# Q and K of a window-attention kernel as three fp32r products each, with the rounding on GpSimd

## The reference, cut to what matters

```python
x = _L0_conv_ref(x, ...)                     # 1x1, grouped 3x3, 1x1 convolution, residual, relu
y = _ln(x, norm1_w, norm1_b)                 # per position, over 128 channels
win = ...                                    # rolled by 3, cut into windows of 7 x 7 = 49 positions
qkv = (win @ qkv_w.T).reshape(B * nW, N, 3, h, d).transpose(2, 0, 3, 1, 4)    # 8 heads of 16
q, k, v = (qkv[0], qkv[1], qkv[2])
attn = jnp.einsum('bhnd,bhmd->bhnm', q, k) * scale + bias + mask
attn = jax.nn.softmax(attn, axis=-1)
out = jnp.einsum('bhnm,bhmd->bhnd', attn, v) @ proj_w.T + proj_b
x = shortcut + out
z = _ln(x, norm2_w, norm2_b)
return x + jax.nn.gelu(z @ fc1_w.T + fc1_b, approximate=False) @ fc2_w.T + fc2_b
```

## Time and profile before

| | |
|---|---|
| median of three runs | 4525.73 us |
| the profiled execution, its own time | 4518.32 us |
| its span in the profile | 4516.2 us |
| PE busy, share of the span | 98% |
| ACT, DVE, POOL busy | 76%, 70%, 49% |
| granted PE clock, mean | 0.992 |

### The profile page before, as it was taken

How to read it: one execution, slowest core, us unless ns; L and a number is a source line. 1 busy time by engine, 2 the same in 40 slices (tenths; PEclk the granted TensorE clock), 3 DMA queues, 4 the chain that set the end, 5 groups by cost and what they waited for, 6 DMA issues and landing times.

```text
span 4516.2 us, 192181 instructions
## 1 busy us (share of the span) xinstructions
PE 4423.1 (98%) x71190; PEld 3178.5 (70%) x71190; DVE 3178.4 (70%) x7717; ACT 3415.4 (76%) x5644; POOL 2207.9 (49%) x3242
## 2 busy tenths in 40 slices
PE   8999996999999999999999999999999999999998
PEld 5666665677777777777777777777777777777775
DVE  4444444777777777777777777777777777777775
ACT  3444443888888888888888888888888888888886
POOL 4444442455554545455555555455555545455553
PEclk9999998999999999999999999999999999999999
DMA  4545442011111111111111111111111111111110
GB/s 138 153 151 163 151 153 66 25 30 29 29 29 30 30 29 29 29 30 29 29 29 30 30 29 29 29 30 29 29 29 29 29 29 29 30 30 29 29 29 26
DMA packets 298330, 218.64 MB, mean 48 GB/s; under 512 B 43377, under 2 KB 245518, under 8 KB 298190
## 3 DMA queue, kind: packets, MB, share of 16 engines
q1 hardware_dynamic: 294632, 215.41, 16.4%
q10 hardware_dynamic: 3558, 1.07, 0.1%
HBM read 110.73 MB, written 111.94 MB: 49 GB/s over the span
## 4 chain that ended last, share of the span: by engine, by line
PE 97%; DVE 1%; issue 1%; ACT 0%; POOL 0%; DMA 0%; DVEq 0%; POOLq 0%; ACTq 0%
PE bank L666 16%; PE bank L608 10%; PE bank L585 8%; PE bank L509 6%; PE bank L576 6%; PE bank L641 6%; PE bank L657 6%; PE bank L595 6%; PE bank L567 5%; PE bank L620 5%; PE bank L522 5%; PE bank L631 4%; PE bank L659 4%; PE bank L658 4%; PE bank L673 2%; PE bank L487 2%
## 5 line engine op out<-in xcount | busy, mean ns | idle before, releaser
L1234 POOL TENSOR_TENSOR sc<-sc,mx 128x784 f32<-128x784 f32 x512 | 779.2, 1522 | 940.9 <-DVE mx L1068 940.9
L666 PE MATMUL bank<-g,fc_sb 128*128 128x392 f32 x2048 | 785.4, 506 | 0.1
L1221 POOL TENSOR_TENSOR res<-x,projb 98x512 f32<-98x512 f32 x256 | 326.3, 1275 | 804.2 <-DVE x L1104 804.2
L861 ACT ACTIVATE g<-bank,fc1b 128x392 f32<-128x392 f32 x1024 | 560.6, 592 | 172.6 <-PE bank L659 172.6
L1087 DVE SCALAR_TENSOR_TENSOR xn<-x,lnp 98x128 f32<-98x128 f32 x1024 | 292.8, 349 | 491.1 <-POOL lnp L1157 491.1
L608 PEld LDWEIGHTS bank<-ident_sb,sc 128*113 128x113 f32 x4096 | 495.6, 177 | 113.1 <-DVE shared L1038 109.8
L666 PEld LDWEIGHTS bank<-g,fc_sb 128*128 128x128 f32 x2048 | 348.7, 190 | 306.2 <-issue 163.1
L608 PE MATMUL bank<-ident_sb,sc 128*113 128x128 f32 x4096 | 547.8, 277 | 0.1
L1062 DVE TENSOR_TENSOR sc<-bank,shared 128x392 f32<-128x392 f32 x1024 | 528.7, 560 | 2.8 <-PE bank L595 2.8
L1068 DVE TENSOR_REDUCE mx<-sc 128x16 f32<-128x784 f32 x512 | 496.6, 970 | 18.5
L1157 POOL TENSOR_TENSOR lnp<-lnp,half 98x8 f32<-98x8 f32 x518 | 467.7, 924 | 20.3
(11 more groups left out here) (105 smaller groups left out, 8258.3 us busy)
## 6 DMA issues: line engine op xcount, KB each, us to landing
x<-x_scratch SPq DMA_DIRECT2D x768, 49.0 KB
out_x<-y SPq DMA_DIRECT2D x672, 49.0 KB
xc_even<-in_x SPq DMA_DIRECT2D x128, 196.0 KB
shared<-in_x SPq DMA_DIRECT2D x128, 196.0 KB
x_scratch<-xc_even SPq DMA_DIRECT2D x128, 196.0 KB
x_scratch<-shared SPq DMA_DIRECT2D x128, 196.0 KB
x<-x_scratch SPq DMA_DIRECT2D x256, 38.5 KB
out_x<-y SPq DMA_DIRECT2D x224, 38.5 KB
```

Source lines behind the costliest of these rows:

```text
L666: mm = nc.tensor.matmul(RC[:, 0:ST], fc2[:, c, :], g[:, c], start=c == 0, stop=c == HC - 1)
L861: nc.scalar.activation(g[:, j], ring[:, 0:ST], ACT.Gelu, bias=fc1b[:, j:j + 1]).then_inc(out_, 1)
L1234: P.tensor_tensor(out=s_r, in0=s_r, in1=m_r.to_broadcast([128, 2 * HEADS, N]), op=ALU.subtract).then_inc(sub_done, 1)
```

## The change

- The normed input `xt` gets a high part `xt_hi`, rounded to fp32r by POOL (`xt_round`, a multiplication by one), and a low part `xt_lo = xt - xt_hi` by DVE (`xt_rest`). The weights of Q and K get theirs once, in the preparation.
- K and Q are three fp32r products each: high by high, low weight by high, high weight by low.
- V is still one fp32 product from `xt`. On PE it moves ahead of K; K moves behind the transposition of z, and Q follows right behind K, into bank 0 of the scores, which is free then. DVE takes Q out of there.
- On ACT, V goes ahead of `zt_hi`, K behind it, and the first two gelu go ahead of the first two pieces of the probabilities.

```diff
-        A_JOBS = 3
+        A_JOBS = 2
...
             def values(t, j):
 
                 if j == 0:
+                    pe.wait_ge(a_out, A_JOBS * t.n + 1)
                     wait(pe, b_out[0], 5 * t.n - 3)
...
-            def project(t, i):
-
-                part = 1 - i
-                wait(pe, a_out, A_JOBS * t.n + 1 + i)
-                nc.tensor.matmul(RA[:, 0:ST], wqkv[:, C * part:C * part + C], xt[:],
-                                 start=True, stop=True).then_inc(a_full, 1)
+            def split_product(dst, part):
+                cols = slice(C * part, C * part + C)
+                nc.tensor.matmul(dst, wqk_hi[:, cols], xt_hi[:], start=True, stop=False)
+                nc.tensor.matmul(dst, wqk_lo[:, cols], xt_hi[:], start=False, stop=False)
+                return nc.tensor.matmul(dst, wqk_hi[:, cols], xt_lo[:], start=False, stop=True)
+
+            def project_k(t):
+                pe.wait_ge(a_out, A_JOBS * t.n + 1)
+                pe.wait_ge(xt_split, t.n + 1)
+                split_product(RA[:, 0:ST], 1).then_inc(a_full, 1)
+
+            def project_q(t):
+
+                wait(pe, s_out, QUADS * t.n)
+                split_product(bank[0][:, 0:ST], 0).then_inc(q_full, 1)
 
             def scores(t, i):
 
-                pe.wait_ge(a_out, A_JOBS * t.n + 3)
+                pe.wait_ge(a_out, A_JOBS * t.n + 2)
+                pe.wait_ge(q_sb, t.n + 1)
...
                 if t.there():
-                    project(t, 0)
                     values(t, 0)
                     values(t, 1)
...
                     to_channels(RC, z, c_full)
                 if t.there():
-                    project(t, 1)
+                    project_k(t)
+                    project_q(t)
...
                 if t.there():
-                    k_out(t)
                     v_out(t)
                 if t3.there():
                     zt_out(t3)
+                if t.there():
+                    k_out(t)
                 if t3.there():
                     nc.scalar.preload_act_table_set("gelu_and_others")
+                if t3.there():
+                    gelu(t3, 0)
+                    gelu(t3, 1)
                 if t1.there():
                     pt_out(t1, 0)
                     pt_out(t1, 1)
                 if t3.there():
-                    gelu(t3, 0)
-                    gelu(t3, 1)
                     gelu(t3, 2)
...
+                    step("wqk_hi", V.tensor_copy, wqk_hi[:], wqkv[:, 0:2 * C])
+                    step("wqk_lo", V.tensor_tensor, out=wqk_lo[:], in0=wqkv[:, 0:2 * C], in1=wqk_hi[:].bitcast(fp32),
+                         op=ALU.subtract)
...
+            def xt_rest(t):
+                dve.wait_ge(xt_rounded, t.n + 1)
+                V.tensor_tensor(out=xt_lo[:], in0=xt[:].rearrange("c w n -> c (w n)"), in1=xt_hi[:].bitcast(fp32),
+                                op=ALU.subtract).then_inc(xt_split, 1)
...
                 if t3.there():
                     y_sum(t3)
+                if ahead.there():
+                    xt_rest(ahead)
                 if t1.there():
                     x2_out(t1)
...
+            def xt_round(t):
+                pool.wait_ge(a_out, A_JOBS * t.n + 1)
+                wait(pool, q_full, t.n)
+                x_ = xt[:].rearrange("c w n -> c (w n)")
+                tt(xt_hi[:], x_, one[:].to_broadcast([C, ST]), ALU.mult).then_inc(xt_rounded, 1)
...
                 if t.there():
                     subtract(t)
+                if ahead.there():
+                    xt_round(ahead)
```

More of the change, by code:

```diff
@@ L141 @@
              "sign", "scaled", "exponent", "power", "signed", "tab", "tab_ps", "tab_rows", "hidden_ps", "hidden", "table_ps", "table",
-             "fc1b_ps", "fc1b", "fc1_scaled", "fc1_hi", "fc1_lo"]
+             "fc1b_ps", "fc1b", "fc1_scaled", "fc1_hi", "fc1_lo", "wqk_hi", "wqk_lo"]
 PREP = CONV_PREP + BIAS_PREP
@@ L185, in program @@
         fc1_hi, fc1_lo = [sb(f"fc1_{i}", [C, HID], fp32r) for i in ("hi", "lo")]
+        wqk_hi, wqk_lo = [sb(f"wqk_{i}", [C, 2 * C], fp32r) for i in ("hi", "lo")]
         fc2 = sb("fc2_sb", [128, HC, C])
         half = sb("half", [128, C])
+        one = sb("one", [128, 1])
         quarter = sb("quarter", [PT, 2, PAIRS])
@@ L221, in program @@
         xt = sb("xt", [C, WINS, N])
+        xt_hi, xt_lo = [sb(f"xt_{i}", [C, ST], fp32r) for i in ("hi", "lo")]
         qt = sb("qt", [C, WINS, QROWS])
@@ L255, in program @@
         zt_split = sem("zt_split")
+        xt_rounded, xt_split, q_full, q_sb = sem("xt_rounded"), sem("xt_split"), sem("q_full"), sem("q_sb")
         conv2_begun, vb_clear = sem("conv2_begun"), sem("vb_clear")
@@ L1041, in q_out @@
             def q_out(t):
-                dve.wait_ge(a_full, A_JOBS * t.n + 3)
+                dve.wait_ge(q_full, t.n + 1)
                 wait(dve, s_full, t.n)
-                V.tensor_copy(qt[:, :, 0:N], RA[:, 0:ST].rearrange("c (w n) -> c w n", n=N)).then_inc(a_out, 1)
+                V.tensor_copy(qt[:, :, 0:N], bank[0][:, 0:ST].rearrange("c (w n) -> c w n", n=N)).then_inc(q_sb, 1)
+            def xt_rest(t):
+                dve.wait_ge(xt_rounded, t.n + 1)
+                V.tensor_tensor(out=xt_lo[:], in0=xt[:].rearrange("c w n -> c (w n)"), in1=xt_hi[:].bitcast(fp32),
+                                op=ALU.subtract).then_inc(xt_split, 1)
             def zt_rest(t):
@@ L1157, in tt @@
                 return P.tensor_tensor(out=o, in0=x, in1=y_, op=op)
+            P.memset(one[:], 1.0)
             step("half", P.memset, half[:], -0.5)
```

## The result

The changed kernel takes 4747.4 us (median of four runs) against 4525.8 us: a ratio of 1.0489, 95% interval 1.0473 to 1.0504. It is slower, as forecast, but by 222 us and not by 97, and outside the range (4588 to 4685).

The account below looks back on a forecast made before the run. Two chains of the same length, PE's and DVE's, were taken to bound each step up to the probabilities. DVE's growth of 0.38 us times 253 gave +96 us, plus 1 us of preparation: 4623 us, range 4588 to 4685.

Parts of the forecast that it names:

- PE's saving is worth nothing as long as DVE's chain ends at P: K and Q on PE fall from 1.45 to 1.23 us, 0.22 us a step, without gain while DVE's v_out sets P.
- P: Mark in each step: the start of the probabilities on PE, at 3008.26 before the change.
- E: Mark in each step: the end of the attention, where xn's transposition starts on PE, at 3003.54 before the change.
- `xt_rest` adds 0.36 to 0.43 us to the chain: On DVE between y and x2, ahead of v_out: the chain grows by 0.36 to 0.43 us a step, 0.38 taken.
- POOL is in time: POOL's `xt_round` ends at 3005.75 to 3005.91, so DVE's `xt_rest` can start at 3005.79 to 3005.95.
- z beside POOL costs nothing: z's norm on DVE while POOL runs `xt_round`: no delay was counted, though the Trainium skill's rule was named against it.
- the forecast's sum: Whole kernel: 253 x 0.38 = +96 us, +1 us of preparation, giving 4623 us for the median.
- rival 2: DVE's z and POOL's xt_round delay each other, overlap 0.40 us: 4703 to 4723 us; 12%, together with a 1275 ns POOL operation.
- z stretched beside POOL: Sign against the forecast: z on DVE or the new POOL operation stretched beside each other; no size given.
- From P to E nothing changes: The stretch from P to the next E, 9.79 us with PE alone, keeps its distances.
- Everything else keeps its cover: Other moved work, such as K's operands, zt_lo and the gelu, costs nothing; DVE's 0.95 us idle ahead of ot stays.

## Why the prediction was wrong

- *PE's saving is worth nothing as long as DVE's chain ends at P.* Right: with that chain unchanged the saving gave 12 us (4513.9), none of them from E to P; with it shortened about 40 (4484.3).
- *`xt_rest` adds 0.36 to 0.43 us to the chain.* Right, 0.36 in the changed kernel and in the one where ACT rounds; alone it is 76 us of the 222.
- *POOL is in time.* Right: xt_hi takes 0.94 us beside z and 0.84 us elsewhere, where 0.87 to 1.03 was priced, and it ended at 3008.62, while DVE was still at z. `xt_lo` waited for it 3 times in all.
- *z beside POOL costs nothing in the forecast's sum, and 0.40 us in rival 2.* This is the step that failed, twice over. It belonged in the sum. The Trainium skill (GPSIMD Engine Reference, "Specifications") names DVE instructions with two SBUF inputs as contending with GpSimd, and z is one. The runs agree with the rule, 134 us for the meeting alone. I had left it at 12%, because I held that no row showed such a meeting, and that reading of the trace was wrong. In the steady steps there is no such pair, but the start of the stage has two. The first xn of all starts inside residual1, and takes 1.34 us where the median is 0.35:

```profile
749.60 1.34 DVE L1087 SCALAR_TENSOR_TENSOR xn<-x,lnp 98x128 f32<-98x128 f32 x1 [3.73 <-POOL lnp L1157]
```
```profile
749.53 1.26 POOL L1221 TENSOR_TENSOR res<-x,projb 98x512 f32<-98x512 f32 x1
```

  It ends at 750.94, 0.15 us behind POOL's end, the same as z in the changed kernel. One z there (796.06, 0.59 us long) starts inside a subtraction and also ends 0.15 us behind it. The size failed with it: it was taken from the overlap of POOL with an undelayed z. From the row above, with POOL's end as forecast, z would have ended at 3004.88 + 0.87 + 0.15 = 3005.90 in place of 3005.36, 0.54 us later; the step would have grown by 0.38 + 0.54 = 0.92 us and the sum been 4525.7 + 253 x 0.92 + 1 = 4759 us, 12 us above what was measured. The delay of z was measured as 0.58 us. The prediction had named z stretched beside POOL as a sign of being wrong, and that is what came.
- *From P to E nothing changes.* Off by 0.06 us a step, in the kernel's favour.
- *Everything else keeps its cover.* Right in the changed kernel (ot's idle time is 0.92 us). Once the statistics stand ahead of zt_lo its cover goes: 0.16 us a step on the kernel before (1.11 against 0.95), and PE's wait at L672 on the changed one.

## What to carry to other kernels

Where the chain shows one engine at 97%, look at the weight loads and short waits beside it: a second engine may end every step at the same moment, and then work taken from the first gives nothing and work put on the second costs in full. When work goes to GpSimd, list which VectorE instructions will be under way in that window. One of z's or `xt_lo`'s kind that starts while GpSimd is inside an instruction should be priced to end behind GpSimd's end, here by 0.15 us at 128 columns and 0.42 at 392; then put the stand into the sum, not into a rival. And before saying that no row shows a pair, look at the longest duration of the line over the whole trace, not at the median or at a steady step: here 1340 ns beside a median of 347 told both that the two meet and what it costs.

## What the runs showed of the hardware

- A scalar_tensor_tensor of 98x128 (broadcast second tensor, fp32, SBUF to SBUF) on VectorE that starts inside a GpSimd instruction ends 0.15 us behind GpSimd's end, whatever GpSimd's length: 0.93 us beside 0.94, and z's total 2.29 us beside 1.57. A tensor_scalar with two columns ends 0.08 us behind it. Between two GpSimd instructions it gets in.
- `xt_lo`, a tensor with a tensor from SBUF, 392 columns, stands too. In the first two strips of the changed kernel, where it meets residual1, it takes 1.6 us and not 0.55, and ends 0.42 us behind GpSimd's end.
- GpSimd stands for VectorE as well. The first xt_lo of the changed kernel and GpSimd behind it:

```profile
760.59 1.62 DVE L1068 TENSOR_TENSOR xt_lo<-xt,xt_hi 128x392 fp32r<-128x392 f32 x1 [2.00 <-POOL xt_hi L1184]
```
```profile
760.52 1.27 POOL L1249 TENSOR_TENSOR res<-x,projb 98x512 f32<-98x512 f32 x1
761.74 0.87 POOL L1184 TENSOR_TENSOR lnp<-st 98x8 f32<-98x8 f32 x3
```

  The three small operations take 0.55 us in the steady steps; here they take 0.87, and the first of them ends at 762.28, 0.07 us behind xt_lo.
- Not all kinds do. The statistics (one SBUF operand) at 3010.48 run beside GpSimd's residual1 and take 0.87 us for four, as in the earlier trace rows. In the trace of the kernel before the maxima (one SBUF operand) take 0.97 us and the scores' bias (one operand in PSUM, one in SBUF) 0.56 us, whether they start inside a GpSimd instruction or meet none. Why tensor_scalar with one SBUF tensor stands and these do not is not shown.
- GpSimd's multiplication of 392 columns by one repeated value takes 0.84 us alone, 784 columns 1.52 us in the kernel's own subtraction, so about 1.73 ns a column and 0.16 us fixed, an estimate from two operations. Beside z the multiplication takes 0.94 us for 392 columns and 1.57 for 784.
